# A graph network kernel: results put out tile by tile, a tail without preparations, and the maximum's addresses at a unit's head

## The reference

```python
w_m = (efeat @ W_msg + b_msg).reshape(E, 16, 16)      # E = 103125 edges
w_a = (efeat @ W_attn + b_attn).reshape(E, 16, 16)
h_src = feat[src][:, :, None]
e1, e2 = w_m * h_src, w_a * h_src
seg_max = segment_max(e2, dst)
ex = exp(e2 - seg_max[dst])
attn = ex / segment_sum(ex, dst)[dst]
ft = segment_sum(e1 * attn, dst).sum(axis=1)          # one row of 16 per node
out = layernorm(x + ft)
```

## Time and profile before

| | us |
|---|---|
| median of 3 runs (2642.5 to 2649.0) | 2643.93 |
| the profiled execution's own time | 2653.84 |
| its span, first to last instruction | 2652.0 |
| first `weighted`, unit 0 | starts 900.59 |
| last `weighted`, unit 115 | starts 2589.04 |
| first of the 25 scatters | starts 2605.05 |
| load of `ft_nat` issued | 2637.82 |

### The profile page before, as it was taken

One profiled execution on the slowest core, in us unless ns is written; L12 is line 12 of the kernel. 1 busy time (PEld: TensorE's weight loads), 2 busy tenths in 40 slices (PEclk: granted clock), 3 DMA queues, 4 the chain that ended last, 5 costly groups with the idle time before them and its releaser, 6 DMA issues.

```text
span 2652.0 us, 38454 instructions
## 1 busy us (share of the span) xinstructions
PE 1889.6 (71%) x5872; PEld 711.2 (27%) x5873; DVE 2005.1 (76%) x3290; ACT 1480.2 (56%) x5083; POOL 1323.4 (50%) x1556
## 2 busy tenths in 40 slices
PE   2446666477982587787777777778787888788872
PEld 1111111132341133233333333323333333333330
DVE  5778999652011588888888888888888898888883
ACT  5134544110001577677777767677777777677762
POOL 2200000315556565656666656656666666566653
PEclk9788988788975699999999999999999898999986
DMA  2010000000001000000000000000000000000010
GB/s 31 16 27 0 0 0 0 2 10 18 11 12 15 9 10 10 9 10 9 10 9 10 10 9 10 9 10 9 10 9 10 9 10 9 10 9 10 9 9 9
DMA packets 87258, 26.30 MB, mean 10 GB/s; under 512 B 63118, under 2 KB 84224, under 8 KB 87104
## 3 DMA queue, kind: packets, MB, share of 16 engines
q0 software_dynamic: 37824, 18.62, 5.9%
q1 hardware_dynamic: 49327, 6.96, 1.7%
q10 hardware_dynamic: 80, 0.43, 0.1%
HBM read 23.30 MB, written 2.51 MB: 10 GB/s over the span
## 4 chain that ended last, share of the span: by engine, by line
issue 30%; DVE 23%; PE 23%; DVEq 16%; ACT 4%; POOL 2%; DMA 1%; another core or an unknown queue 0%; ACTq 0%; PEldq 0%; POOLq 0%; PEld 0%
PE pair L808 9%; DVE eo L1434 6%; DVE hot L1162 4%; DVEq L1453 3%; ACT eo L997 3%; PE pw L699 3%; PE pw L795 3%; DVE eo L1477 2%; DVE eo L1468 2%; PE pw L696 2%; PE pw L695 2%; DVE top L1449 2%; DVE top L1454 2%; DVE bank L1462 1%; PE pair L804 1%
## 5 line engine op out<-in xcount | busy, mean ns | idle before, releaser
L617 POOL DMA_INDIRECT nbr<-table,rec x960 | 995.2, 1037 | 547.6 <-ACT eo L997 285.1
L808 PE MATMUL pair<-eo,ident 128*128 128x512 f32 x1856 | 886.3, 622 | 10.4 <-issue 7.7
L997 ACT ACTIVATE eo<-pw,nbr 128x32 f32<-128x32 f32 x3776 | 705.5, 370 | 78.7 <-issue 63.2
L1434 DVE TENSOR_TENSOR eo<-pw,nbr 128x1024 f32 (+1 forms) x357 | 423.3, 1218 | 160.8 <-issue 87.3
L795 PE MATMUL pw<-wk,termsT 100*128 100x512 bf16 x954 | 314.7, 416 | 257.9 <-issue 182.4
L808 PEld LDWEIGHTS pair<-eo,ident 128*128 128x128 f32 x1856 | 364.7, 200 | 488.7 <-issue 472.6
L1162 DVE TENSOR_SCALAR hot<-iota_key,near_key 128x500 bf16<-128x500 f16 x974 | 273.5, 345 | 67.7 <-issue 38.9
L986 ACT ACTIVATE eo<-eo 128x2048 f32<-128x2048 f32 x117 | 223.5, 1910 | 105.3 <-DVE eo L1468 75.1
L1468 DVE TENSOR_TENSOR eo<-eo,bank (+1 forms) x117 | 267.6, 2287 | 10.8
L1477 DVE TENSOR_TENSOR eo<-eo x232 | 272.6, 1216 | 3.7 <-issue 3.7
L660 PE MATMUL bank<-hot 128*128 128x500 bf16 x488 | 150.1, 424 | 149.3 <-DVE hot L1162 101.8
(11 more groups left out here) (244 smaller groups left out, 1822.3 us busy)
## 6 DMA issues: line engine op xcount, KB each, us to landing
nbr<-table,rec POOLq DMA_INDIRECT x960
rec<-unit_recs SPq DMA_DIRECT2D x122, 8.0 KB
attr<-in_edge_attr_dram,rec POOLq DMA_INDIRECT x120
unit_recs<-place SPq DMA_DIRECT2D x27, 64.0 KB
shared<-key_row SPq DMA_DIRECT2D x1, 1600.0 KB, 6.5
counts<-in_dst_dram SPq DMA_DIRECT2D x1, 448.0 KB
counts<-in_src_dram SPq DMA_DIRECT2D x1, 448.0 KB
place<-in_src_dram,at_i POOLq DMA_INDIRECT x26, 2.6
```

Source lines behind the costliest of these rows:

```text
L617: pool.indirect_dma_start(nbr[:, b, j * FEAT:(j + 1) * FEAT], None, table, bass.IndirectOffsetOnAxis(ap=rec[:, b, j:j + 1], axis=0)).then_ ...
L808: mm = pe.matmul(total, ident[:], eo[:, ring, j * 2 * CH:(j + 1) * 2 * CH], start=False, stop=(j == SLOT - 1), skip_group_check=True)
L997: done = act.activation(eo[:, ring, lo:lo + wide], pw[:, j - 4, c * wide:(c + 1) * wide], ACT.Copy, scale=nbr[:, held, j * FEAT + c:j * FE ...
L1434: dve.tensor_tensor(eo[:, bass.ds(ring, 1), k * 4 * CH:(k + 1) * 4 * CH] .rearrange("p r (c f) -> p (r c) f", f=2 * FEAT), pw[:, 2 * (k % ...
```

## The change

1. `outcome` signals a new semaphore `s_tile`. POOL's scatter of tile t waits for `s_tile` to reach t + 2 instead of `s_ft`, which only the last one still waits for.
2. POOL's loop has 29 turns instead of 30 and SP's loop 28, followed by four units written out that load no records beyond unit 115. After them SP adds one to `s_attr_ok`, which stands in for the attributes of unit 116.
3. PE's and ACT's loops have 28 turns instead of 29, followed by four units written out, with `ahead` 3, 2, 1 and 0: what would prepare a unit behind 115 is left out.
4. DVE's loop runs over the first 24 tiles. The last tile is written out: a first unit and a loop for what exceeds three units (neither runs here, since the tile has three), then three units with `ahead` 2, 1 and 0. The last has `weighted` and a wait for the sums alone.
5. `peaks` is handed `old` and `new`, snapped at the head of `one_unit`, instead of multiplying `even` and `odd` by 256 itself.
6. The unit count: at least two units to a tile and three in the last. Here nothing changes by it: 116 units. One small instruction and a drain are added in `place_nodes`, and `unit_recs` is 25 records longer.

```diff
@@ sync
+            def records(i, b, load):
+                ahead = (b + 2) % SETS
+                sp.wait_ge(s_attr[b], i * 16 + 16)
+                sp.sem_inc(s_attr_ok, 1)
+                sp.wait_ge(s_nbr[b], i * (16 * SLOT) + 16 * SLOT)
+                sp.sem_inc(s_nbr_ok, 1)
+                if load:
                     sp.wait_ge(s_scaled, i * SETS + b + 3)
...
+            with sp.Fori(0, before_last) as i:
+                for b in range(SETS):
+                    records(i, b, True)
+            for b in range(SETS):
+                records(before_last, b, b < 2)
+            sp.sem_inc(s_attr_ok, 1)
@@ gpsimd
-            quads = pool.value_load(levels[0:1, NT + 1:NT + 2], min_val=1, max_val=MANY)
+            quads = pool.value_load(levels[0:1, NT + 2:NT + 3], min_val=2, max_val=MANY)
...
-            pool.wait_ge(s_ft, 1)
             for t in range(NT):
+                if t < NT - 1:
+                    pool.wait_ge(s_tile, t + 2)
+                else:
+                    pool.wait_ge(s_ft, 1)
                 pool.indirect_dma_start(ft_nat, bass.IndirectOffsetOnAxis(ap=ids[:, t:t + 1], axis=0),
                                         ft_p[:, t + 1, :], None).then_inc(s_out, 16)
@@ tensor
+            def pe_unit(b, u, ahead):
+                sums(b % RING, 0, u)
+                if ahead > 2:
+                    product((b + 3) % 2, 1, u + 3)
+                sums(b % RING, 1, u)
+                if ahead > 3:
+                    turn(b % 2, 0, u + LEAD)
...
+            with pe.Fori(0, before_last) as i:
                 for b in range(SETS):
+                    pe_unit(b, i * SETS + b, LEAD)
+            for b in range(SETS):
+                pe_unit(b, before_last * SETS + b, 3 - b)
@@ scalar
+            def act_unit(b, u, ahead):
+                if ahead > 2:
                     high(b % 2, b, u + LEAD)
+                if ahead > 1:
                     last_pair((b + 2) % RING, (b + 2) % SETS, u + 2)
+                if ahead > 2:
                     middle(b % 2, u + LEAD)
+                if ahead > 0:
                     fading(u + 1)
                     powers((b + 1) % RING, u + 1)
+                if ahead > 3:
                     for half in range(2):
                         turned(b % 2, half, u + LEAD)
@@ vector, peaks and outcome
-                before = bank[0][:, bass.ds(old * CH, CH)]
-                after = bank[0][:, bass.ds(new * CH, CH)]
+                before = bank[0][:, bass.ds(old, CH)]
+                after = bank[0][:, bass.ds(new, CH)]
...
-                                  ratio[:].rearrange("p (i o) -> p o i", o=FEAT), AX_X, ALU.add)
+                                  ratio[:].rearrange("p (i o) -> p o i", o=FEAT), AX_X, ALU.add).then_inc(s_tile, 1)
@@ vector, one_unit
+                old = dve.snap(even * CH, min_val=0, max_val=CH)
+                new = dve.snap(odd * CH, min_val=0, max_val=CH)
...
+                if ahead > 3:
+                    rest_one(even, held, u + LEAD)
+                if ahead > 0:
+                    peaks(following, within, old, new, u + 1, None if tile is None else (tile, odd))
+                if ahead > 3:
+                    rest_two(even, u + LEAD)
+                    scaled(fourth, later, u + 3)
                 dve.reg_add(step, step, 1)
-                accumulate(even, u)
+                if ahead > 0:
+                    accumulate(even, u)
+                else:
+                    dve.wait_ge(s_sum, u + 1)
...
+            with dve.Fori(0, NT - 1) as t:
...
+            with dve.If(n > 3):
+                one_unit(None, NT - 1)
+            with dve.If(n > 4):
+                with dve.Fori(4, n):
+                    one_unit(None, None)
+            one_unit(None, dve.snap(first + (NT - 1), min_val=NT - 1, max_val=NT), 2)
+            one_unit(None, None, 1)
+            one_unit(None, None, 0)
```

More of the change, by code:

```diff
@@ L52 @@
 REC = 16
-UMAX = E // SLOT + NB // SLOT + NT + 4 * SLOT
+UMAX = E // SLOT + NB // SLOT + 2 * NT + 4 * SLOT
 MASKED = -1e30
@@ L462, in _ @@
             sp.wait_ge(s_stage, 1)
-            quads = sp.value_load(levels[0:1, NT + 1:NT + 2], min_val=1, max_val=UMAX // SETS - 2)
+            before_last = sp.value_load(levels[0:1, NT + 1:NT + 2], min_val=1, max_val=UMAX // SETS - 3)
             for b in range(2):
                 sp.dma_start(rec[:, b, :], unit_recs[:, b, :]).then_inc(s_rec[b], 16)
[L466 to L472, removed]
+            def records(i, b, load):
[5 more added lines that the diff above has]
+                if load:
                     sp.wait_ge(s_scaled, i * SETS + b + 3)
@@ L1284, in place_nodes @@
                 dve.tensor_copy(lev_f[:], levels[:, 0:NT])
+                dve.drain()
+                dve.tensor_scalar(lev_f[:, NT - 1:NT], lev_f[:, NT - 1:NT], 3.0, None, ALU.max)
                 dve.drain()
@@ L1296, in place_nodes @@
                 dve.drain()
-                dve.tensor_scalar(levels[:, NT + 1:NT + 2], lev_quad[:], 1.0, None, ALU.add)
+                dve.tensor_scalar(levels[:, NT + 1:NT + 2], lev_quad[:], 1.0, None, ALU.subtract)
                 dve.tensor_scalar(lev_quad[:], lev_quad[:], float(SETS), None, ALU.mult)
@@ L1519, in _ @@
             scaled(2, 2, 2)
-            peaks(0, 0, 1, 0, 0)
+            peaks(0, 0, CH, 0, 0)
             left = dve.alloc_register("dve_left")
@@ L1525, in _, with one_unit @@
             coming = dve.alloc_register("dve_coming")
-            def one_unit(remaining, tile):
+            def one_unit(remaining, tile, ahead=LEAD):
                 u = dve.snap(step, min_val=0, max_val=MANY)
@@ L1536, in one_unit @@
                 fourth = dve.snap((u + 3) % RING, min_val=0, max_val=RING - 1)
-                remaining()
-                dve.reg_alu(left, left, 2, ALU.min)
-                within = dve.snap(dve.snap(left, min_val=1, max_val=2) - 1, min_val=0, max_val=1)
+                if remaining:
+                    remaining()
+                    dve.reg_alu(left, left, 2, ALU.min)
+                    within = dve.snap(dve.snap(left, min_val=1, max_val=2) - 1, min_val=0, max_val=1)
+                else:
+                    within = 1
                 weighted(here, u)
-                if tile is not None:
+                if tile is not None and remaining:
                     dve.reg_mov(coming, dve.value_load(levels[0:1, bass.ds(tile + 1, 1)], min_val=1, max_val=E))
-                rest_one(even, held, u + LEAD)
-                peaks(following, within, even, odd, u + 1, None if tile is None else (tile, odd))
-                rest_two(even, u + LEAD)
-                scaled(fourth, later, u + 3)
-                dve.reg_add(step, step, 1)
-                accumulate(even, u)
-            with dve.Fori(0, NT) as t:
+                if ahead > 3:
+                    rest_one(even, held, u + LEAD)
+                if ahead > 0:
+                    peaks(following, within, old, new, u + 1, None if tile is None else (tile, odd))
+                if ahead > 3:
+                    rest_two(even, u + LEAD)
+                    scaled(fourth, later, u + 3)
+                dve.reg_add(step, step, 1)
+                if ahead > 0:
+                    accumulate(even, u)
+                else:
+                    dve.wait_ge(s_sum, u + 1)
+                    dve.sem_inc(s_settled_dve, 1)
+            with dve.Fori(0, NT - 1) as t:
                 n = dve.snap(units, min_val=1, max_val=E)
@@ L1555, in _ @@
                 dve.reg_add(units, coming, 0)
+            n = dve.snap(units, min_val=3, max_val=E)
+            some = dve.alloc_register("dve_some")
+            dve.reg_sub(left, n, 3)
+            dve.reg_alu(some, left, 1, ALU.min)
+            first = dve.snap(some, min_val=0, max_val=1)
+            with dve.If(n > 3):
[6 more added lines that the diff above has]
+            one_unit(None, None, 0)
             total = dve.snap(step, min_val=1, max_val=MANY)
```

32 lines of the change are left out of this document (15 added, 17 removed).

## The result

The changed kernel takes 2619.9 us (median of 10 runs, 2606.7 to 2632.9), the kernel before beside it on the same chip 2644.8 (2641.4 to 2668.2): ratio 0.9903, 95% interval 0.9873 to 0.9932. It is faster, by 25 us and not by 37.5; the predicted 2606 is 14 us too low and the time lies 0.9 us above the range.

A forecast was written before the change was run, and what follows sets the result against it. It took POOL's row of scatters at the end and DVE's last three units as the bound: 30.7 + 6.8 = 37.5 us off 2643.93 gave 2606.4, say 2606; range 2596 to 2619 us.

The forecast's parts named there:

- The scatters off the path: End of the program on POOL: 24 scatters ahead of the last leave the path, saving 30.66 us.
- If every one of the 23 took 0.87 longer: POOL's early scatters beside DVE: even if stretched, 20 us more, done by 2570 and hidden, so no cost.
- Tail: Units 113 to 115 on DVE without needless preparations: 33.45 instead of 41.90 us, 8.4 saved, 6.8 after 1.6 for TensorE's clock.
- the clock: PE's sums in units 114 and 115 run slower after longer idle times: 0.6 and 1.0 us lost, 1.6 together.
- Unit 112, "they cancel": Work for unit 116 left out on ACT and PE gains 0.2 us; DVE's jumps over unrun parts cost 0.2.
- The new wait on ACT: In unit 112 `high` for unit 116 waits until unit 115's neighbours land: 25 us of cover, no cost.
- the addresses at the head: DVE's 0.36 us gap at the head of `one_unit`: register instructions stay despite the snapped values, so no gain.
- A: Rival: code of the last four units must be fetched first, 4.7 us lost, gain 32.8, time 2611 us; chance 0.15.
- B: Rival: snapped addresses remove 0.36 us from all 116 units, 41.8 us, time 2564, or about 2585; chance 0.02.
- C: Rival: DVE's loop, two instructions further on, loses 0.93 us a turn, 104 us, time 2710; chance 0.03.
- the conditions under which I called the forecast wrong: Scatters waiting for something besides their tile, microsecond gaps at a loop exit, or the mean unit changing by over 0.1 us.
- an unforeseen loss: Whole kernel: a loss not foreseen that leaves a difference within 0.3% of the kernel before; chance 0.02.

The follow-up runs named there:

- the control: The changed kernel run once more, nothing altered: ratio 0.9911 (0.988 to 0.9943) against the kernel before.
- the version without the stall: The changed kernel with its early scatters in four groups of six, POOL waiting for a unit's `weighted` ahead of each: 2599.6 us, ratio 0.9827 against the kernel before.
- the row of 41: 17 gathers and 24 scatters without a break, in the kernel before with only the scatters put out tile by tile: ratio 0.9988.

## Why the prediction was wrong

- **The scatters off the path, 30.66 us**: right, 30.65.
- **"If every one of the 23 took 0.87 longer, it would be 20 us more [...] and still hidden: cost nothing."** This is the step that failed. The scatters weren't stretched: of the 23 only one took 1.90 us, the one that began 0.15 us into `weighted` of unit 111, the others 0.97 to 1.02. What I asked was whether the working engines slow POOL down; I didn't ask what POOL's row does to them. It held up the signals from PE to ACT and DVE and cost 20.5 us in this profile, 21.7 in the control, against the kernel before; 24 to 25 against the same kernel with the scatters at the end or in rows of six. "No other instruction is queued behind them on POOL" was true and beside the point.
- The Trainium skill's rule (SBUF — State Buffer, "SBUF: two separate sides"), that DVE keeps POOL's descriptors waiting, pointed at the same place, but in the other direction: the loss is in DVE and ACT, and nearly all of it with DVE idle.
- **Tail**: 13.47, 11.04, 8.94 forecast before the clock; 13.29, 11.97, 8.81 in the changed kernel, 13.30, 11.03, 8.80 with rows of six. Unit 114 of the first had a granted clock of 0.72, that of the second 0.85, and PE's sixteen matmuls of the sums took 9.74 us and 8.80: the clock took 0.9 us in the first and nothing in the second; I had 1.6. DVE waits 1.84 us for the exponential ahead of `weighted` of unit 114, as forecast; the wait forecast ahead of that of unit 115 stands before `accumulate` instead, 2.94 us for PE.
- **Unit 112, "they cancel"**: a little too careful. 13.10 instead of 14.14 us; where nothing holds them up, units 110 to 112 gain 1 to 3.7 us together, to which the gathers for units that don't exist may add their part. I had seen that POOL issued them and had given their going no value.
- **The new wait on ACT, the addresses at the head**: nothing, as forecast. The gap ahead of L1499 is 0.35 and 0.39 us, as the 0.36 before.
- **Rivals**: A is out (0.32 us ahead of unit 113, where the new code begins). The Trainium skill's rule that was cited beside it (Runtime: NRT & Kernel Launch, "Instruction fetch mechanics"), a stall at a taken branch out of the loaded blocks, shows no cost here: the jump over the parts that don't run lies within these 0.32 us. Whether it leaves the loaded blocks is shown by no run. B is out by the unchanged gaps; C by the loop, whose units 0 to 109 take 1610.2 us where they took 1613.8 before. The loss was one that no rival named; of the conditions under which I called the forecast wrong, none occurred either, but one of the signs that I named for it failed: units 110 and 111 took 27.97 and 24.80 us, outside the 12.7 to 18 us named for units 1 to 112.
- **The range** held "an unforeseen loss" at 2 in 100 and only one so large that it eats the whole gain. A loss of half the gain, in the one piece of work that was moved into a busy stretch, had no room.

By parts the time is 2643.9 - 30.7 - 7.8 + 20.5 = 2626, 6 us above the measured 2620. The measured gain of the version without the stall (0.9827: 46 us) goes 3 us beyond its 43.4 us by the profiles (137.6 - 94.2). The interval of that gain, 35 to 57 us, holds both, and the start of the stage alone varies by 12 us from one execution to the next. For the version with the scatters at the end the profile's 12.8 us lie outside the interval, and that stays open.

## What to carry to other kernels

When transfers are moved off the end of a program into a busy stretch, ask not only whether they are hidden, but what a row of them does to the engines that work there. In this kernel rows of 6 indirect transfers from POOL cost nothing, those of 8 and 9 mostly nothing and at most a wait of 3.1 us, two of 12 came with a loss of 4 us, those of 17 now and then made a wait of up to 5 us, those of 19 and 20 in the loop some of 1.5 to 13, and one of 31 cost 20 to 25. A wait for the next unit behind each six gave back the whole 25 us; with a break of 2.2 us in its place the three units took 43.25 us instead of 41.72. A wait in the profile marked "remote", with the work that it waits for long done, and POOL's timeline at the same microseconds are the two views that show it.

## What the runs showed of the hardware

- A long row of indirect transfers on POOL holds up signals between other engines. In rows of 31, gathers and scatters alike, ACT stood waiting for PE for 7 to 17 us and DVE for 12.5 to 22. In the changed kernel the updates of PE's semaphores stand 7.3 to 13.9 us behind the ends of the instructions that make them. ACT to DVE and ACT's own drain were late too, by about 4 and 5 us, in the row of 41. Some signals within the same rows came through at once (ACT's copy that ended at 2521.72 let PE go on at 2521.86), so it isn't a full stop.
- 56 plain transfers from POOL, 0.53 us each, 29.74 us in a row, held up nothing; nor did 0.95 us memsets.
- The data moved are no measure of it: in the stretch of the 23 scatters the DMA engines were busy for 4% and moved 6 GB/s.
- What in the chip delays the signals is open. It isn't the fetching of instructions: in the changed kernel, in the version with one scatter per turn and in the one with the scatters tile by tile alone no packet of an instruction queue moves in the loop's stretch with the late signals. The rows of 31 held transfers of 128 rows of 64 bytes only; whether larger or smaller ones do the same is open too.
